# Copying the edge blocks of the normalised high bands on ScalarE instead of by transfers, in a wavelet convolution and codebook kernel

## The chip, the cores and the metric

One Trainium2 chip, one core of it. The metric is the device time of one execution in microseconds (us). The kernel before takes 2009.77 us, the median of 3 runs (2007.31 to 2010.28).

## What is computed

The input x has 8 images of 128x128 pixels with 32 channels. Two residual stages follow each other. The first normalises each channel over its image, splits the result into four half-size Haar bands, and runs three convolution branches over the three high bands:

```python
LL, LH, HL, HH = _dwt_haar(x)
hf = jnp.concatenate([LH, HL, HH], axis=-1)
x1 = _lrelu(_conv(_lrelu(_conv(hf, w15, b15)), w25, b25))
x2 = _lrelu(_conv(_lrelu(_conv(hf, w13, b13)), w23, b23))
x3 = _lrelu(_conv(_lrelu(_conv(hf, w12, b12)), w22, b22))
added = x1 + x2 + x3
y = ...                      # wd1, wd2, wd3: 3x3 convolutions, dilated by 2
alpha = jax.nn.sigmoid(_conv(y, wca, bca))
phf = alpha * hf
z = ...                      # wcb (3x3) over [LL, phf], batch norm, z * sigmoid(z)
phf2 = _conv(phf, whf, bhf)
return _idwt_haar(pLL, phf2, HL, HH)
```

The second stage normalises again and adds, for each pixel, the nearest of 512 codebook rows (argmin of the distance over 32 dimensions):

```python
x = x + _L0_conv_ref(_gn(x), ...)
x = x + _L1_conv_ref(_gn(x), L1_conv_codebook)
```

## The kernel before, in words

A half-size band is 64x64 pixels of 32 channels. On the chip a band is a tile of 128 partitions, four neighbouring columns by 32 channels, with 16 such blocks of columns (JN) by 64 rows along the free dimension, and two rows of zeros at each end. A convolution is a sum of 128x128 matrices (`wring`, `wfull`) times such a tile, shifted by rows: the matrix mixes the four columns of a block. For columns that lie in the neighbouring block there is a second tile, the EDGE tile: its lower 64 partitions hold two columns of the next block, its upper 64 two of the block before. The 5x5 convolution w15 over the three high bands reads both, OWN and EDGE.

The three high bands are kept as a rounded part and a rest, so that TensorE can multiply in its quick format (fp32r) and still be exact enough: `hf[m][kind][low]`, with m the band (3), kind OWN or EDGE, low 0 or 1, all in the one buffer `hfp`. ScalarE writes the rounded OWN parts (`normal_own`, L1174, semaphore s_hfw), VectorE the rests (`normal_low`, L1358, semaphore s_hfl), both at the end of the image before. SyncE makes the EDGE tiles by transfers within SBUF (`edges_of`, L740).

The kernel runs three images at once, in `rounds`: in round b it does the convolutions of image b, the codebook search of image b-1 (128 score products called "tile", L884, then MAX8 L1484 and FIND_INDEX8 L1488 on VectorE, then a gather of codebook rows by GpSimd, L1603), and the transform of image b+1 (transposes L816, copy L1151, Haar sums L1300 to L1305). All engines walk the same list `PLAN`, 610 steps, each doing at a step what is its part: the order of work is thus fixed for every engine, and semaphores tie them. `("mm", ...)` is one matrix product; ("tile", t), ("ychunk", c), ("xchunk", c) and ("edge", m) are set between products. The three edge steps stand at 49, 56 and 63 units of the plan's own account of TensorE (`AT`): edge 0 right behind the first product of w22, edge 1 and 2 within the OWN products of w15. The products of w15 that read EDGE tiles begin behind all 90 OWN products.

Behind the last product of a group (convolution and half) ScalarE evacuates the PSUM bank to `z` (L1044), adding the bias, and frees the bank (s_free); VectorE then applies the leaky ReLU from `z` (L1368), waiting for s_free. For w22 VectorE adds the two branches right behind it (L1374). ScalarE also does, from round to round: `lln`, the normalised low band, and its sides (L1168, L1181), at the step edge 1; the codebook search's operands, `high` (L1083) and `stack_high` (L1100), which tiles eight steps later read; and the copies of ychunk (L1162) and xchunk (L1151) that free score banks. There are four score banks, handed out in turn: a tile's product waits (`bank_free`) until the user four turns before has been read.

TensorE waits for the EDGE tiles in `inputs_ready`, at the first EDGE product of each band: L906.

```python
EDGES = ((slice(0, P // 2), slice(1, JN), slice(0, JN - 1)),
         (slice(P // 2, P), slice(0, JN - 1), slice(1, JN)))
AT = {("edge", 0): 49, ("edge", 1): 56, ("edge", 2): 63,
      ("upper",): 191, ("xsquare", 0): 137}
```

Of the kernel before, what the change touches and what calls it, by code (L numbers as in the profile page):

```python
# [14 lines left out]
ROWS = HEIGHT // 2  # L15
# [3 lines left out]
PAD = 2  # L19
# [47 lines left out]
OWN, EDGE, LEFT, RIGHT = range(4)  # L67
# [349 lines left out]
for _i, _x in enumerate(PLAN):  # L417
    if _x[0] == "mm":
# [15 lines left out]
EDGES = ((slice(0, P // 2), slice(1, JN), slice(0, JN - 1)),  # L434
         (slice(P // 2, P), slice(0, JN - 1), slice(1, JN)))
# [14 lines left out]
def conv_vq_kernel(nc, x, weights, params, codes4, codebook, ident, group_mean, part_mask, out):  # L450
    ctx = ExitStack()
    with ctx:
# [3 lines left out]
        def sem(name):  # L456
            return ctx.enter_context(nc.semaphore(name))
# [32 lines left out]
        hf = [[[hfp[:, m, kind, low] for low in range(2)] for kind in range(2)] for m in range(3)]  # L490
# [49 lines left out]
        s_hfl = sem("s_hfl")  # L540
        s_hfe = [sem(f"s_hfe{m}") for m in range(3)]
# [24 lines left out]
        s_hfw = sem("s_hfw")  # L566
# [73 lines left out]
        def raw(par, slot):  # L640

            return bands[par][:, slot // 2, :, slot % 2, :]
# [32 lines left out]
        def _(sp):  # L675
# [46 lines left out]
            def block_rows(tile, rows, js):  # L722

                return tile[rows, js].rearrange("p j i -> p (j i)").bitcast(F32)
# [7 lines left out]
                            sp.dma_start(block_rows(side[to][low], slice(q * CH, (q + 1) * CH), dst),  # L732
                                         block_rows(hf[q][OWN][low], near, src)).then_inc(s_side[low], 16)

            def edges_of(n, m):

                for low, ready in enumerate((s_hfw, s_hfl)):
                    sp.wait_ge(ready, 3 * n + m + 1)
                    for p, src, dst in EDGES:
                        sp.dma_start(block_rows(hf[m][EDGE][low], p, dst), block_rows(hf[m][OWN][low], p, src))\  # L740
                            .then_inc(s_hfe[m], 16)

            def keep_page(p):

                if PARTED[p]:
# [20 lines left out]
            def body(b, par, conv, quant, nxt):  # L766
                v = b - 1
                if conv and b:
                    sides_of(b)
                for i, step in enumerate(PLAN):  # L770
                    what = step[0]
                    if quant and what == "var2":
                        stack(v, 0)
                    elif quant and what == "bias2":
                        stack(v, 1)
                    elif quant and what == "tile":
                        t = step[1]
                        if t % JTILES == 0 and t >= JTILES and t // JTILES + 1 < JN:
                            stack(v, t // JTILES + 1)
                        if t == 7 and v:  # L780
                            store(v - 1, XCHUNKS - 1)
                        if t % CTILES == 15 and t > CTILES:
                            store(v, t // CTILES - 1)
                    elif v > 0 and what == "late" and step[1] == TILES - 1:
                        store(v - 1, XCHUNKS - 2)
                    elif conv and what == "edge":
                        edges_of(b, step[1])
                    elif nxt and what == "xchunk":
                        ahead = XCHUNKS * (b + 1) + step[1] + 2
                        if ahead < XCHUNKS * IMAGES:  # L790
                            load(ahead // XCHUNKS, ahead % XCHUNKS)
                    if conv and i in PAGE_AFTER:
                        p = PAGE_AFTER[i] + NR
                        page(NP * b + p)
                        if b == 0 and p < NP and PARTED[p]:
                            keep_page(p)
                            raw_page(SPLIT_PAGES.index(p) + 2)
                if b > IMAGES:
                    store(v - 1, XCHUNKS - 1)
# [13 lines left out]
        def _(pe):  # L813
# [86 lines left out]
            def inputs_ready(b, n, half, m, kind, low):  # L900

                if n in SPLIT:
                    if half == 0 and n == "w13" and kind == OWN:
                        pe.wait_ge(s_hfl if low else s_hfw, 3 * b + m + 1)
                    elif half == 0 and n == "w15" and kind == EDGE:
                        pe.wait_ge(s_hfe[m], 64 * (b + 1))  # L906
                    elif half == 0 and n == "w13" and kind == LEFT:
                        pe.wait_ge(s_side[low], 96 * (b + 1))
                elif n in MAKER and m == 0:
                    if kind == 0:  # L910
                        pe.wait_ge(s_leaky, len(LEAKY) * 2 * b + GROUP[MAKER[n], half] + 1)
                    elif half == 0:
                        pe.wait_ge(s_edge, len(HAS_EDGE) * b + HAS_EDGE.index(MAKER[n]) + 1)
                elif n == "wd1":
                    if kind == 0:
                        pe.wait_ge(s_sum, 2 * b + half + 1)
                    elif half == 0:
                        pe.wait_ge(s_yedge, b + 1)
                elif n == "wcb":
                    if kind != OWN:  # L920
                        if kind == LEFT and half == 0:
                            pe.wait_ge(s_pside, b + 1)
                    elif m == 0:
                        if half == 0:
                            pe.wait_ge(s_lln, b + 1)
                    else:
                        pe.wait_ge(s_phf, 6 * b + 2 * (m - 1) + half + 1)
                elif n == "whf" and m == 2:
                    pe.wait_ge(s_phf, 6 * b + 2 * m + half + 1)
# [84 lines left out]
        def _(act):  # L1014
# [150 lines left out]
            def normal_ll(n, par):  # L1165

                wait(act, s_cbmap, 4 * (n - 1) + 1)
                nc.scalar.activation(lln[:, :, PAD:PAD + ROWS], raw(par, LL), ACT.Identity, bias=shift1[:, :],  # L1168
                                     scale=scale1[:, :]).then_inc(s_lln, 1)

            def normal_own(n, par, m):
# [2 lines left out]
                nc.scalar.activation(hf[m][OWN][0][:, :, PAD:PAD + ROWS], raw(par, BANDS[m]), ACT.Identity,  # L1174
                                     bias=0.0, scale=scale1[:, :]).then_inc(s_hfw, 1)

            def ll_sides(n):

                act.wait_ge(s_lln, n + 1)
                for to, near, src, dst in SIDES:  # L1180
                    nc.scalar.copy(pside[to][SIDE_LL * CH:P, dst, PAD:PAD + ROWS],  # L1181
                                   lln[near, src, PAD:PAD + ROWS])
# [8 lines left out]
            def body(b, par, conv, quant, nxt):  # L1191
                v = b - 1
                for i, step in enumerate(PLAN):
                    what = step[0]
                    if nxt and b and i == 0:
                        for k in range(2):
                            xorder(b + 1, k)
                    if quant and what == "var2":
                        for j in range(2):
                            high(v, 1 - par, j)  # L1200
                        for part in (0, 2):
                            stack_high(v, 1 - par, 0, part)
                    elif quant and what == "bias2":
                        code_parts(v)
                    elif quant and what == "tile":
                        j, k = step[1] // JTILES, step[1] % JTILES
                        if k in (1, 3) and j + 1 < JN:
                            stack_high(v, 1 - par, j + 1, k - 1)
                        if k == 0 and j + 2 < JN:
                            high(v, 1 - par, j + 2)  # L1210
                    elif quant and what == "ychunk":
                        ycopy(v, step[1])
                    elif nxt and what == "xchunk":
                        xcopy(b + 1, step[1], BANK[step])
                    elif conv and what == "edge" and step[1] == 1:
                        normal_ll(b, par)
                        ll_sides(b)
                    elif nxt and what == "xsquare":
                        x_squares(b + 1, 1 - par, step[1])
                    elif conv and what == "wside":  # L1220
                        weighted_side(b, step[1])
                    elif conv and what == "mm":
                        for key, (_, last) in SPAN.items():
                            if last == i:
                                evacuate(b, key)
                                if key == ("wcb", 0):
                                    low_square(b, par)
                                if key in RESTORE:
                                    restore(b, par, RESTORE.index(key))
                    if nxt and i == LOW_AT:  # L1230
                        for m in range(3):
                            normal_own(b + 1, 1 - par, m)
# [541 lines left out]
```

## Time and profile before

| what | value |
|---|---|
| median of the runs | 2009.77 us |
| the profiled execution's own time | 2006.41 us |
| its span, first to last instruction | 2004.6 us |
| mean granted clock of TensorE | 0.943 |
| TensorE (PE) busy | 1855.6 us, 93% |
| VectorE (DVE) busy | 1763.2 us, 88% |
| GpSimd (POOL) busy | 1258.9 us, 63% |
| ScalarE (ACT) busy | 1011.8 us, 50% |
| transfers | 197.21 MB, mean 98 GB/s |
| the chain that ended last | PE 50%, DVE 30%, POOL 8%, issue 6%, ACT 5% |

A share of busy time is a mean over the span. The kernel has a start of about 120 us without any codebook search, eight rounds of convolutions of some 226 us each, and a tail with search alone. In a timeline a row is: start in us, length in us, engine, line, operation, what it writes and reads, how many in a row, and in brackets the idle time of the engine just before it and who ended it. An ACT row without brackets came right behind the row before; an instruction begins about 0.1 us before its predecessor's recorded end, where they are of one engine and nothing is waited for.

### The profile page before, as it was taken

What the parts mean: (1) busy time and instruction counts of PE and PEld (TensorE: products, weight loads), DVE (VectorE), ACT (ScalarE), POOL (GpSimd) and SP (SyncE); (2) the same over time, 40 slices, a digit from 0 to 9 for tenths busy, and PEclk for the clock granted to TensorE, in tenths of its full rate; (3) what the DMA queues carried; (4) which work ended last, traced back from release to release, by engine and by line L of the source; (5) the groups of instructions that cost most, each with busy time, mean ns of one, the idle gap of its engine ahead of it and who ended that gap; (6) DMA issues with size and microseconds to landing.
All of it is one profiled execution on the core that took longest, in us unless ns stands there. A gap on an engine that the chain in (4) does not pass through costs nothing.

```text
span 2004.6 us, 22679 instructions
## 1 busy us (share of the span) xinstructions
PE 1855.6 (93%) x6112; PEld 1117.6 (56%) x6112; DVE 1763.2 (88%) x3947; ACT 1011.8 (50%) x2034; POOL 1258.9 (63%) x1363
## 2 busy tenths in 40 slices
PE   7999999999999999999999999999999999985553
PEld 5654666456754666456754666556754666432221
DVE  5312799999999999999999999999999999989896
ACT  3325464646457464655456464655456353634331
POOL 1001367756778567766777567766677567767876
PEclk8999999999999999999999999999999999995555
DMA  6621463234622463234532463234532453201111
GB/s 193 189 71 48 112 161 90 70 91 123 156 77 69 115 160 100 71 88 123 156 81 70 116 156 103 71 87 125 155 82 60 107 148 94 61 19 34 35 39 31
DMA packets 135023, 197.21 MB, mean 98 GB/s; under 512 B 36976, under 2 KB 82544, under 8 KB 134896
## 3 DMA queue, kind: packets, MB, share of 16 engines
q1 hardware_dynamic: 101808, 178.40, 31.9%
q0 software_dynamic: 32768, 16.84, 5.4%
q8 instruction: 49, 0.80, 0.2%
q14 instruction: 78, 0.64, 0.1%
q10 hardware_dynamic: 320, 0.52, 0.1%
HBM read 117.52 MB, written 23.72 MB: 70 GB/s over the span
## 4 chain that ended last, share of the span: by engine, by line
PE 50%; DVE 30%; POOL 8%; issue 6%; ACT 5%; ACTq 0%; DMA 0%; POOLq 0%; DVEq 0%
PE ring L959 42%; DVE idx L1488 11%; DVE top L1484 10%; POOL vqc L1603 7%; PE score L884 6%; PE score L816 1%; ACT yst L1100 1%; ACT ha L1032 1%; DVE bands L1305 1%; POOL vqc L1617 1%; DVE hfp L1358 1%; DVE brs L1368 1%; DVE bands L1423 1%; DVE bands L1419 1%; POOL yl L1611 1%
## 5 line engine op out<-in xcount | busy, mean ns | idle before, releaser
L1603 POOL DMA_INDIRECT vqc<-in_codebook,idx x1024 | 999.4, 976 | 454.7 <-DVE idx L1488 259.4
L1484 DVE MAX8 top<-score 128x8 f32<-128x512 f32 x1024 | 690.2, 684 | 47.5 <-PE score L884 29.5
L884 PE MATMUL score<-cst,yst 98*128 98x512 f32 x1024 | 621.2, 612 | 90.8 <-DVE idx L1488 69.9
L1488 DVE FIND_INDEX8 idx<-top,score 128x8 uint32<-128x512 f32 x1024 | 703.2, 691 | 0.0
L959 PE MATMUL ring<-hfp,wring 128*128 128x512 f32 x2160 | 596.5, 411 | 3.0 <-ACT hfp L1174 3.0
L959 PEld LDWEIGHTS ring<-hfp,wring 128*128 128x128 f32 x2160 | 411.3, 191 | 116.2 <-issue 10.7
L1100 ACT CAST yst<-bands 32x256 fp32r<-32x256 f32 x1024 | 411.7, 402 | 100.9 <-PE score L884 88.6
L959 PE MATMUL ring<-ha,wfull 128*128 128x512 f32 x896 | 439.2, 597 | 5.2 <-POOL ha L1635 4.7
L884 PEld LDWEIGHTS score<-cst,yst 98*128 98x128 f32 x1024 | 205.4, 203 | 296.7 <-DVE idx L1488 176.0
L959 PE MATMUL ring<-hb,wfull 128*128 128x512 f32 x736 | 356.7, 595 | 0.0
L959 PEld LDWEIGHTS ring<-ha,wfull 128*128 128x128 f32 x896 | 168.9, 190 | 149.4 <-issue 126.3
L959 PEld LDWEIGHTS ring<-hb,wfull 128*128 128x128 f32 x736 | 138.8, 190 | 128.1 <-issue 118.2
L1044 ACT ACTIVATE z<-ring,prm 128x512 f32<-128x512 f32 x144 | 98.8, 687 | 191.9 <-PE ring L959 188.8
L1162 ACT COPY ync<-score 128x256 f32<-128x256 f32 x128 | 41.4, 375 | 229.4 <-PE score L816 148.0
L1611 POOL TENSOR_TENSOR yl<-bands,yh 128x256 fp32r<-128x256 f32 x128 | 96.6, 757 | 15.8 <-ACT yh L1083 14.0
L1635 POOL TENSOR_TENSOR ha<-ha,brs 128x512 f32<-128x512 f32 x16 | 17.5, 1116 | 140.7 <-ACT brs L1061 140.6
L959 PE MATMUL ring<-sidep,wring 96*128 96x512 f32 x384 | 103.6, 405 | 0.0
L1083 ACT CAST yh<-bands 128x256 fp32r<-128x256 f32 x128 | 51.1, 405 | 84.5 <-DVE bands L1423 83.5
L959 PE MATMUL ring<-pside,wfull 128*128 128x512 f32 x192 | 85.9, 596 | 0.0
L1151 ACT COPY xt<-score 128x512 f32<-128x512 f32 x64 | 37.1, 582 | 93.8 <-PE score L816 71.0
L959 PEld LDWEIGHTS ring<-sidep,wring 96*128 96x128 f32 x384 | 72.7, 189 | 20.2
L1617 POOL TENSOR_TENSOR vqc<-vqc,ync 128x512 f32<-128x512 f32 x64 | 82.1, 1283 | 2.7 <-DMA vqc<-in_codebook,idx 1.6
(138 smaller groups left out, 1327.5 us busy)
## 6 DMA issues: line engine op xcount, KB each, us to landing
wring<-wparts SPq DMA_DIRECT2D x119, 384.0 KB, 3.3
hfp<-hfp SPq DMA_DIRECT2D x96, 255.0 KB, 5.2
yst<-yl SPq DMA_DIRECT2D x512, 32.0 KB
vqc<-in_codebook,idx POOLq DMA_INDIRECT x1024
out<-vqc SPq DMA_DIRECT2D x128, 128.0 KB
xnat<-in_x SPq DMA_DIRECT2D x112, 128.0 KB, 3.1
wfull<-in_weights SPq DMA_DIRECT2D x32, 384.0 KB
sidep<-hfp SPq DMA_DIRECT2D x96, 127.5 KB, 3.1
```

The costliest lines, as they stand in the source:

```text
L884: nc.tensor.matmul(score[bank][:, :], yst[0:KST, j % 2, g, wp], cst[0:KST, :], start=True, stop=True).then_inc(s_tile, 1)
L959: t = nc.tensor.matmul(ring[GBANK[key]][:, :, :], w[rows], src[rows], start=(i == first), stop=(i == last))
L1044: nc.scalar.activation(z[:, g % 2], bank[:, :, :], ACT.Identity, bias=col("b" + n[1:]))\
L1083: nc.scalar.copy(yh[:, j % 2], block_of(par, j)).then_inc(s_yh, 1)
L1100: t = nc.scalar.copy(yst[part * CH:(part + 1) * CH, j % 2, g], block_of(par, j, slice(g * CH, (g + 1) * CH)))
L1151: nc.scalar.copy(xt[:, k % 2].rearrange("p w j e i -> p (w j e i)"), score[bank][:, :])\
L1162: t = nc.scalar.copy(dst[:, j], src[:, j])
L1484: nc.vector.max(top8[:, t % 4, :], score[bank][:, :]).then_inc(s_top, 1)
L1488: nc.vector.max_index(idx[:, t // CTILES % 2, t % CTILES, :], top8[:, t % 4, :], score[bank][:, :]).then_inc(s_idx, 1)
L1603: nc.gpsimd.indirect_dma_start(vqc[:, c % 2, w * CH:(w + 1) * CH], None, codebook[:, :], bass.IndirectOffsetOnAxis(idx[:, c % 2, k, 0:1], ...
L1611: nc.gpsimd.tensor_tensor(yl[:, j % 2], bands[par][:, :, j].rearrange("p w e i -> p w (e i)"), yh[:, j % 2], ALU.subtract).then_inc(s_yl, 1)
L1617: nc.gpsimd.tensor_tensor(vqc[:, c % 2, :], vqc[:, c % 2, :], ync[:, c % 2, :], ALU.add)\
```

## The change

ScalarE copies the EDGE tiles, four copies of 64 partitions x 15 blocks x 64 rows for each band: two halves of the tile, for the rounded part and for the rest. SyncE's twelve transfers per image are gone, and so is `edges_of`. s_hfe[m] now counts one per image and band, where it counted 64. ScalarE waits for s_hfl, the rests of that band.

```diff
-            def edges_of(n, m):
-
-                for low, ready in enumerate((s_hfw, s_hfl)):
-                    sp.wait_ge(ready, 3 * n + m + 1)
-                    for p, src, dst in EDGES:
-                        sp.dma_start(block_rows(hf[m][EDGE][low], p, dst), block_rows(hf[m][OWN][low], p, src))\
-                            .then_inc(s_hfe[m], 16)
-
...
-                    elif conv and what == "edge":
-                        edges_of(b, step[1])
...
-                        pe.wait_ge(s_hfe[m], 64 * (b + 1))
+                        pe.wait_ge(s_hfe[m], b + 1)
...
+            def high_edges(n, m):
+
+                act.wait_ge(s_hfl, 3 * n + m + 1)
+                for low in range(2):
+                    for p, src, dst in EDGES:
+                        t = nc.scalar.copy(hf[m][EDGE][low][p, dst, PAD:PAD + ROWS],
+                                           hf[m][OWN][low][p, src, PAD:PAD + ROWS])
+                t.then_inc(s_hfe[m], 1)
+
...
-                    elif conv and what == "edge" and step[1] == 1:
-                        normal_ll(b, par)
-                        ll_sides(b)
+                    elif conv and what == "edge":
+                        high_edges(b, step[1])
+                        if step[1] == 1:
+                            normal_ll(b, par)
+                            ll_sides(b)
```

ScalarE's queue in a middle round, from the evacuation of w23's first half on to the copy of ychunk 2. Before:

```order
L1044 ACTIVATE z<-ring,prm 128x512 [waits s_leaky,s_grp]
L1151 COPY xt<-score 128x512 [waits s_dwt,s_xT]
L1145 COPY xord<-xnat 128x256 [waits s_x1,s_xT]
L1145 COPY xord<-xnat 128x256
L1044 ACTIVATE z<-ring,prm 128x512 [waits s_leaky,s_grp] x3
L1168 ACTIVATE lln<-bands,shift,scale 128x16x64 [waits s_cbmap]
L1181 COPY pside<-lln 32x15x64 [waits s_lln]
L1181 COPY pside<-lln 32x15x64
L1083 CAST yh<-bands 128x256 [waits s_yl,s_band]
L1100 CAST yst<-bands 32x256 [waits s_tile]
L1100 CAST yst<-bands 32x256 x3
```

After (line numbers of ScalarE's part are 10 lower up to `normal_own`, 1 lower behind it; L1172 is the new copy):

```order
L1034 ACTIVATE z<-ring,prm 128x512 [waits s_leaky,s_grp]
L1172 COPY hfp<-hfp 64x15x64 [waits s_hfl]
L1172 COPY hfp<-hfp 64x15x64 x3
L1034 ACTIVATE z<-ring,prm 128x512 [waits s_leaky,s_grp] x2
L1172 COPY hfp<-hfp 64x15x64 [waits s_hfl]
L1172 COPY hfp<-hfp 64x15x64 x3
L1158 ACTIVATE lln<-bands,shift,scale 128x16x64 [waits s_cbmap]
L1180 COPY pside<-lln 32x15x64 [waits s_lln]
L1180 COPY pside<-lln 32x15x64
```

The three evacuations in a row (w23's second half, w22's two halves) are now parted behind the first by four copies; four more stand ahead of the low band, and the last four behind the next eight `yst` casts and ahead of the copy of ychunk 2:

```order
L1090 CAST yst<-bands 32x256 [waits s_tile]
L1090 CAST yst<-bands 32x256 x3
L1172 COPY hfp<-hfp 64x15x64 [waits s_hfl]
L1172 COPY hfp<-hfp 64x15x64 x3
L1152 COPY ync<-score 128x2x4x32 [waits s_add,s_yT]
L1152 COPY ync<-score 128x2x4x32
```

SyncE's queue at the same place. Before:

```order
L740 DMA hfp<-hfp 64x1020 [waits s_hfw]
L740 DMA hfp<-hfp 64x1020
L740 DMA hfp<-hfp 64x1020 [waits s_hfl]
L740 DMA hfp<-hfp 64x1020
L764 DMA wring<-wparts 128x768 [waits s_kept0,s_grp]
L740 DMA hfp<-hfp 64x1020 [waits s_hfw]
L740 DMA hfp<-hfp 64x1020
L740 DMA hfp<-hfp 64x1020 [waits s_hfl]
L740 DMA hfp<-hfp 64x1020
L719 DMA yst<-yl 32x256 [waits s_yl,s_tile]
```

After:

```order
L756 DMA wring<-wparts 128x768 [waits s_kept0,s_grp]
L719 DMA yst<-yl 32x256 [waits s_yl,s_tile]
L719 DMA yst<-yl 32x256 x3
L756 DMA wring<-wparts 128x768 [waits s_kept1,s_mark]
L756 DMA wring<-wparts 128x768 [waits s_kept2,s_mark]
```

The weight pages (`wring<-wparts`) and the operand transfers (`yst<-yl`) now stand directly behind one another. TensorE's, VectorE's and GpSimd's queues keep their order.

## Rows read from the trace of the kernel before

**Rows 1.** Page, busy time by engine, and the chain that ended last.

```profile
PE 1855.6 (93%) x6112; PEld 1117.6 (56%) x6112; DVE 1763.2 (88%) x3947; ACT 1011.8 (50%) x2034; POOL 1258.9 (63%) x1363
PE 50%; DVE 30%; POOL 8%; issue 6%; ACT 5%; ACTq 0%; DMA 0%; POOLq 0%; DVEq 0%
```

**Rows 2.** Windows of round 4: length, busy PE, PEld, DVE, ACT, POOL; clock, DMA share.

```profile
955.00:965.00 10.00, 10.00 (x44) 7.92 (x43) 10.00 (x24) 4.69 (x11) 6.10 (x7) 1.00 0.96 248
1000.00:1040.00 40.00, 39.98 (x125) 22.03 (x124) 38.76 (x88) 19.70 (x40) 29.97 (x31) 1.00 0.31 80
```

**Rows 3.** Timeline of ACT in round 4, 936 to 967 us.

```profile
936.18 4.05 ACT L1032 COPY ha<-ha 32x960 f32<-32x960 f32 x4
940.25 2.03 ACT L1032 COPY hb<-hb 32x960 f32<-32x960 f32 x2
...
946.47 0.69 ACT L1044 ACTIVATE z<-ring,prm 128x512 f32<-128x512 f32 x1
...
948.14 0.70 ACT L1044 ACTIVATE z<-ring,prm 128x512 f32<-128x512 f32 x1
949.67 0.69 ACT L1044 ACTIVATE z<-ring,prm 128x512 f32<-128x512 f32 x1 [0.84 <-PE ring L959]
952.28 0.69 ACT L1044 ACTIVATE z<-ring,prm 128x512 f32<-128x512 f32 x1 [1.92 <-PE ring L959]
952.87 1.24 ACT L1168 ACTIVATE lln<-bands,shift,scale 128x1024 f32<-128x1024 f32 x1
...
956.18 0.41 ACT L1083 CAST yh<-bands 128x256 fp32r<-128x256 f32 x1
956.49 3.31 ACT L1100 CAST yst<-bands 32x256 fp32r<-32x256 f32 x8
966.35 0.65 ACT L1162 COPY ync<-score 128x256 f32<-128x256 f32 x2 [6.54 <-PE score L816]
```

**Rows 4.** Groups by line and form, ACT: copies of the new shape, writers of hfp.

```profile
L1021 ACT COPY ha<-ha 64x960 f32<-64x960 f32 x32 | 32.3, 1009 | 18.7 <-DVE ha L1368 18.5
L1174 ACT ACTIVATE hfp<-bands,scale 128x1024 fp32r<-128x1024 f32 x24 | 25.9, 1143 | 48.9 <-DVE shift L1338 48.9
```

**Rows 5.** Timeline of DVE in round 4, then round 1, then round 7.

```profile
947.20 0.69 DVE L1368 SCALAR_TENSOR_TENSOR brs<-z 128x512 f32<-128x512 f32 x1 [1.09 <-ACT z L1044]
952.87 0.69 DVE L1368 SCALAR_TENSOR_TENSOR brs<-z 128x512 f32<-128x512 f32 x1
...
269.68 0.69 DVE L1368 SCALAR_TENSOR_TENSOR brs<-z 128x512 f32<-128x512 f32 x1
...
1629.44 0.67 DVE L1368 SCALAR_TENSOR_TENSOR brs<-z 128x512 f32<-128x512 f32 x1
1644.43 0.70 DVE L1484 MAX8 top<-score 128x8 f32<-128x512 f32 x1 [0.25 <-PE score L884]
```

**Rows 6.** Timeline of PE: the wait for DVE in round 4 and in round 7.

```profile
967.64 0.50 PE L884 MATMUL score<-cst,yst 98*128 98x512 f32 x1 [0.26 <-DVE idx L1488]
970.41 0.40 PE L884 MATMUL score<-cst,yst 98*128 98x512 f32 x1
...
1649.64 0.51 PE L884 MATMUL score<-cst,yst 98*128 98x512 f32 x1 [0.22 <-DVE idx L1488]
```

**Rows 7.** Timeline of ACT: w23's last evacuation in rounds 1 and 7.

```profile
264.95 0.70 ACT L1044 ACTIVATE z<-ring,prm 128x512 f32<-128x512 f32 x1
1624.70 1.26 ACT L1044 ACTIVATE z<-ring,prm 128x512 f32<-128x512 f32 x2
```

**Rows 8.** Timeline of DVE in round 0: the next wait behind w22.

```profile
79.82 0.36 DVE L1348 CAST wring<-ync 128x384 fp32r<-128x384 f32 x1 [1.14 <-PE ring L959]
```

**Rows 9.** Timeline of POOL in round 4; then its waits for a DMA.

```profile
961.22 0.75 POOL L1611 TENSOR_TENSOR yl<-bands,yh 128x256 fp32r<-128x256 f32 x1
POOL vqc L1617 <- DMA vqc<-in_codebook,idx: 1.6, 1, 1.6
POOL vqc L1603 <- DMA out<-vqc: 1.4, 1, 1.4
```

## The prediction

> **What bounds the kernel now.** I read the page first. TensorE is busy for 93% of the span, VectorE for 88%, ScalarE for 50%, and the chain that ended last runs through TensorE for 50% and through VectorE for 30%; transfers have 0% of it [rows 1]. So neither the removed transfers nor ScalarE, which gets the work, looks like the bound. The windows of a middle round show the two that are: from 955 to 965 us VectorE and TensorE are both busy for all 10.00 us, and from 1000 to 1040 TensorE for 39.98 of 40 [rows 2]. Two engines are nearly full and hold each other up in turn. A delay of either that is not taken up before the other waits for it goes into the end time, and once in every round. The question is therefore not how much ScalarE has to do, but whether VectorE or TensorE comes to wait for it at the three places where the copies stand.
>
> The timelines of ScalarE, VectorE and TensorE between 936 and 972 us answer that. VectorE does the leaky ReLU of w22's first half at 952.87 us, without any wait ahead of it [rows 5]: `z` had been ready since 949.67 + 0.69 = 950.36 [rows 3]. From there on it has no gap, until at 967.64 us TensorE waits 0.26 us for it, since all four score banks are full [rows 6]. So between 952.87 and 967.64 VectorE sets the pace, and behind it TensorE does, with hardly a gap up to 1040.
>
> **The change, part by part.** A copy of 64x960 takes 1009 ns on ScalarE [rows 4], and four in a row 4.05 us, with the next instruction 4.07 us behind the first's start [rows 3]. There are 3 x 4 x 8 = 96, so ScalarE gets 96 x 1.009 = 97 us more work, 1109 us in all or 55%. By itself that costs nothing.
>
> *Edge 0.* The copies stand between the evacuations of w23's second half and w22's first half. The former starts at 948.14 us; whatever follows it without a wait starts 0.59 us later (as 952.28 and 952.87 show) [rows 3]. Four copies put the evacuation of w22 to 948.14 + 0.59 + 4.07 = 952.80 instead of 949.67. VectorE's leaky ReLU starts 0.73 us behind its evacuation (946.47 to 947.20) [rows 3, 5], so at 953.53 instead of 952.87: it is late by 0.66 us. TensorE itself doesn't care: the banks that w15 takes next were freed by w23's two evacuations, which stand ahead of the copies. The second half of w22 was evacuated at 952.28 and now goes at about 953.4, while VectorE is busy with the first half and the sum of the branches, so nothing comes on top. Round 1 gives the same: 264.95 + 5.39 = 270.34 against 269.68, again 0.66 [rows 5, 7]. The plan is the same in rounds 1 to 6, which makes **6 x 0.66 = 4.0 us**.
>
> VectorE has no gap in the next 15 us to take that up in, and TensorE already waits for it at 967.64, so the wait there becomes 0.9 us and the 0.66 us goes into the end in full.
>
> *Round 7* has no transform of a next image, so VectorE comes to w22 sooner. The second of the two evacuations that start at 1624.70 begins at 1625.28; 1625.28 + 5.39 = 1630.67 against 1629.44, 1.23 us late [rows 5, 7]. VectorE has a gap of 0.25 us at 1644.43, ahead of TensorE's wait at 1649.64 [rows 5, 6], so **1.0 us** is left.
>
> *Round 0* has no search. `z` of w22 comes 2.4 us later than VectorE wants it, but VectorE waits 1.14 us for TensorE at 79.82 and over 3 us at each of the next three weight pages [rows 8], and the split pages run some pages ahead of their use. Nothing, unless that lead is smaller than it looks.
>
> *Edge 1* adds 4.07 us ahead of the low band. Going down ScalarE's queue with the lengths of the rows: w22's second evacuation 953.4 to 954.1, four copies to 958.0, `lln` and its sides to 961.35, `yh` to 961.8, eight `yst` casts to 965.0 (they ended at 959.8) [rows 3]. GpSimd wants that `yh` at 961.22, and itself comes 0.66 later now, at 961.88 [rows 9]: just in time. The tile that reads the `yst` stands behind the transposes of ychunk 2, just over 966 us. Nothing, with 0.1 us to spare at the first place and over 1 us at the second.
>
> *Edge 2* then runs from 965.0 to 968.9 and puts the copy of ychunk 2 from 966.35 to 968.9, ready at 969.6. Its score bank is wanted four turns later, by the product at 970.41 [rows 6], which itself is 0.66 later. Nothing, with 1.5 us to spare. Behind it ScalarE has gaps again and catches up. The first EDGE product of w15 stands 90 products and some 20 tiles behind 951.7, at about 977.5 us; the copies are done by 968.9, so the new form of that wait isn't felt either.
>
> *Removed.* SyncE issues 12 x 8 = 96 transfers less. They ran where the transfer engines were fullest, at a share of 0.96 [rows 2]. But no row of the steady rounds shows TensorE or VectorE waiting for a transfer; the only waits of GpSimd for one are 1.6 and 1.4 us in the whole run [rows 9]. I put the relief at nothing, with 3.0 us as its bound.
>
> **The sum** is 4.0 + 1.0 = 5.0 us, against the profiled execution's 2006.41: 2011.4. That execution is 3.4 us under the median of the runs shown, so in the terms of the median 2009.77 + 5.0 = **2014.8 us**, 0.25% more.
>
> The unknown price is that of the copy, which no row shows from `hfp` to `hfp` in fp32r. The nearest row by shape, partitions and operation is the 1009 ns that I take. The far bound is what ScalarE's writer of `hfp` takes, 1143 ns for 1024 columns and 128 partitions [rows 4]: then edge 0 is late by 4 x 0.134 = 0.54 more in seven rounds, and the sum is 5.0 + 3.8 = 8.8 us, or 2018.5. On the other side, without the 3.0 us of waits for transfers, it is 2.0 us, or 2011.8. The Trainium skill (VectorE: DVE Perf Modes, the section on the TRN2 errata) gives a ScalarE copy within SBUF 224 cycles plus one per element at 1.2 GHz: that is (224 + 960) / 1.2 = 987 ns, an estimate from that page, against the trace's 1009. By it edge 0 would be late by 0.57 us and the sum 4.4 us, just above what a measurement can tell; the trace's duration is used.
>
> **The rivals.** *Paid back* (not slower): the end hardly moves, because the delay of 0.66 us and a relief of transfers cancel. For it speaks the DMA share of 0.96 just there: the transfers that carry weight pages and `yst` now start up to 3 us sooner. Against it speaks that their readers did not wait. The most that it gives back is 3.0 of 5.0 us; if VectorE's delay were also met by gaps that the modelled ends of the products hide, nothing would be left: 2009.8 to 2011.8.
>
> *A score bank comes late* (slower still): with longer copies edge 2 pushes the copy of ychunk 2 beyond the turn of its bank. From 1.24 us a copy on (what `lln` takes) twelve copies are 12 x 0.23 = 2.8 us longer, the bank is free at 972.3 against a wish at 970.41 + 0.66 + 0.92 = 971.99, and each round loses 0.92 us at edge 0 and 0.35 at the bank: 5.0 + 7 x 1.27 = 13.9, or 2023.7. It decides from about 1.2 us a copy; below, the bank is free in time.
>
> *The transfers did hold something up* (faster): they take bandwidth from the gathers or slow the engines' own reads, and the end moves below 2005.8. Against it, no such wait is in the rows beyond the 3.0 us, which even alone, with no delay at edge 0, would give 2006.8. The Trainium skill (SBUF — State Buffer, Who interferes with whom) says that a DMA never contends with a compute engine for SBUF; by that rule nothing at all is gained there.
>
> **How the numbers follow.** A measurement of this kernel tells about 0.2% from no change, 4.0 us here. The forecast case has 0.58; since 5.0 lies only 1.0 above the bound, 0.13 of it would come out as "same". Paid back has 0.24, the late bank 0.10, the faster case 0.08. That gives slower 0.45 + 0.10 = 0.55, same 0.13 + 0.24 = 0.37, faster 0.08. The range goes from 2008.5 (paid back, with about a microsecond for the run) to 2019.0 (the far bound of the copy), and leaves out most of the late bank and of the faster case.
>
> **What would show it.** Right: 96 copies `hfp<-hfp` of 1.01 us and ScalarE near 1109 us; a wait of VectorE for `z` of about 0.66 us at w22's first half in rounds 1 to 6, where there was none, and of about 1.2 in round 7; TensorE's wait at the second tile behind ychunk 2 grown from 0.26 to 0.9 us; rounds 0.66 us longer. Wrong: rounds of the old length though VectorE waits (then it was taken up, and the place of that gap tells where); copies well over 1.01 us; a wait of TensorE for ync or `yst` around 965 to 972 us; or a wait of GpSimd for `yh` that VectorE then shows.

## The result, and the profile after

The changed kernel takes 2013.96 us (median of 19 runs, 2012.44 to 2016.08) against 2010.0 us for the kernel before, measured beside it in as many runs (2006.29 to 2013.02). The ratio is 1.0021, with a 95% interval of 1.0014 to 1.0027: slower by 4.0 us, where 5.0 had been forecast.

The page of the profiled execution, busy time by engine and the chain that ended last, answers to [rows 1]:

```profile
PE 1863.4 (93%) x6112; PEld 1118.2 (56%) x6112; DVE 1763.5 (88%) x3947; ACT 1107.2 (55%) x2130; POOL 1259.0 (63%) x1363
PE 50%; DVE 29%; POOL 8%; ACT 7%; issue 6%; ACTq 0%; DMA 0%; POOLq 0%; DVEq 0%
```

ScalarE is busy 95 us more, 1107.2 where 1109 was forecast, and TensorE 8 us more; the others are as before. The groups by line and form name the new copy (partitions x elements, count, busy us, mean ns, idle time ahead):

```profile
L1172 ACT CAST hfp<-hfp 64x960 fp32r<-64x960 f32 x96 | 97.1, 1011 | 1.0
```

It takes 1011 ns where 1009 was taken from [rows 4]. The timeline of ScalarE in round 4, to be laid beside [rows 3]:

```profile
951.35 0.69 ACT L1034 ACTIVATE z<-ring,prm 128x512 f32<-128x512 f32 x1
951.94 0.58 ACT L1141 COPY xt<-score 128x512 f32<-128x512 f32 x1
952.40 0.72 ACT L1135 COPY xord<-xnat 128x256 f32<-128x256 f32 x2
953.02 0.69 ACT L1034 ACTIVATE z<-ring,prm 128x512 f32<-128x512 f32 x1
953.60 4.06 ACT L1172 CAST hfp<-hfp 64x960 fp32r<-64x960 f32 x4
957.68 1.27 ACT L1034 ACTIVATE z<-ring,prm 128x512 f32<-128x512 f32 x2
958.84 4.09 ACT L1172 CAST hfp<-hfp 64x960 fp32r<-64x960 f32 x4
962.95 1.25 ACT L1158 ACTIVATE lln<-bands,shift,scale 128x1024 f32<-128x1024 f32 x1
...
966.27 0.41 ACT L1073 CAST yh<-bands 128x256 fp32r<-128x256 f32 x1
966.58 3.32 ACT L1090 CAST yst<-bands 32x256 fp32r<-32x256 f32 x8
969.92 4.09 ACT L1172 CAST hfp<-hfp 64x960 fp32r<-64x960 f32 x4
974.04 0.65 ACT L1152 COPY ync<-score 128x256 f32<-128x256 f32 x2
...
1010.18 0.69 ACT L1034 ACTIVATE z<-ring,prm 128x512 f32<-128x512 f32 x1 [2.88 <-PE ring L949]
```

From 953.02 on ScalarE has no gap at all up to the copy of ychunk 2. The evacuation of w22's first half starts 4.66 us behind that of w23's second half; before it was 1.53 us behind. And VectorE in the same round, and in round 7:

```profile
952.07 0.69 DVE L1369 SCALAR_TENSOR_TENSOR brs<-z 128x512 f32<-128x512 f32 x1 [1.09 <-ACT z L1034]
958.40 0.69 DVE L1369 SCALAR_TENSOR_TENSOR brs<-z 128x512 f32<-128x512 f32 x1 [0.58 <-ACT z L1034]
959.73 0.68 DVE L1369 SCALAR_TENSOR_TENSOR brs<-z 128x512 f32<-128x512 f32 x1
...
1639.27 0.69 DVE L1369 SCALAR_TENSOR_TENSOR brs<-z 128x512 f32<-128x512 f32 x1 [1.12 <-ACT z L1034]
```

The wait of 0.58 us at w22's first half is new; rounds 1 to 6 all show it. Its second half, at 959.73, is not waited for.

How long a delay lasts is best read between two fixed points of a round: from the evacuation of w23's first half to that of w15's first half, four evacuations later, 951.35 to 1010.18 here. I call this stretch S and use it below. It is 58.83 us after, and was 58.17 before: from 946.47 [rows 3] to the evacuation in this row of the kernel before.

```profile
1004.64 0.69 ACT L1044 ACTIVATE z<-ring,prm 128x512 f32<-128x512 f32 x1 [2.88 <-PE ring L959]
```

In rounds 1 to 5 it is 58.16 or 58.17 before and 58.81 or 58.82 after; in round 7 56.75 and 57.58. In round 0 it is 49.00 in both, though VectorE waits there for w22's first half too, 2.33 us: the waits of 1.14 and 3.28 us for TensorE that came behind it have shrunk to none and 2.41.

The profiled executions differ by more than the medians: their spans are 2004.6 and 2013.8 us, 9.2 us apart. Seven stretches S account for 5.3 of it (0.66 in rounds 1 to 5, 1.16 in round 6, 0.83 in round 7). Of the 1.16 only about 0.65 belongs to the change: in round 6 VectorE also waits for GpSimd (its `vqc`), 0.69 us in the kernel before and 1.17 in the changed one, but 1.18 and 1.23 us in e3 and e1 below too, which lose nothing. The rest is not in the places that the change touches. In round 0, between w15's first evacuation and the next round's, the kernel after takes 147.67 us and the one before 146.21, with as many products. Windows of that stretch, after and then before (length, busy us of PE, PEld, DVE, ACT, POOL, granted clock, DMA share):

```profile
117.88:265.55 147.67, 145.89 (x438) 79.87 (x437) 71.56 (x144) 72.87 (x122) 30.67 (x35) 0.99 0.27 75
```

```profile
117.08:263.29 146.21, 144.43 (x438) 78.82 (x437) 71.42 (x144) 72.88 (x122) 30.59 (x35) 1.00 0.29 79
```

The clock was lower for a moment, and a narrow window of the kernel after shows where:

```profile
225.00:232.00 7.00, 5.22 (x23) 3.69 (x22) 2.60 (x5) 6.37 (x17) 1.69 (x6) 1.00 0.43 135
232.00:236.00 4.00, 4.00 (x12) 3.12 (x11) 2.65 (x5) 2.06 (x6) 0.19 (x1) 0.57 0.09 27
```

From 232 to 236 us the granted clock is 0.57, that is mostly at 1.2 GHz, right behind 7 us in which TensorE was busy for 5.22 only; elsewhere in the stretch it is 2.4 GHz. Such a piece costs 1.5 us here. The profiled execution before has three in its steady rounds, this one six, and e1 and e3 below, whose times are those of the kernel before, have three and six. So of the 9.2 us about 5 are the change and about 4, by three more drops at 1.3 to 1.5 us, are an estimate for the clock; the medians of 19 runs are 4.0 us apart.

### The profile page after: what moved, and what is told of

The parts are those of the page before. It is cut to its first block, busy times and chain, and to the rows that moved or that the text cites. A ratio compares the mean times of both kernels' runs of the same rounds, so it can differ in the third digit from the quotient of the medians.

```text
span 2013.8 us, 22679 instructions
## 1 busy us (share of the span) xinstructions
PE 1863.4 (93%) x6112; PEld 1118.2 (56%) x6112; DVE 1763.5 (88%) x3947; ACT 1107.2 (55%) x2130; POOL 1259.0 (63%) x1363
## 4 chain that ended last, share of the span: by engine, by line
PE 50%; DVE 29%; POOL 8%; ACT 7%; issue 6%; ACTq 0%; DMA 0%; POOLq 0%; DVEq 0%
PE ring L949 41%; DVE idx L1489 11%; DVE top L1485 10%; POOL vqc L1604 6%; PE score L874 6%; PE score L806 1%; ACT yst L1090 1%; ACT ha L1022 1%; ACT hfp L1172 1%; DVE hfp L1359 1%; DVE bands L1306 1%; POOL vqc L1618 1%; DVE bands L1424 1%; ACT z L1034 1%; DVE bands L1420 1%
## 5 line engine op out<-in xcount | busy, mean ns | idle before, releaser
L1172 ACT CAST hfp<-hfp 64x960 fp32r<-64x960 f32 x96 | 97.1, 1011 | 1.0
```

What stands on the lines that cost most here:

```text
L1172: t = nc.scalar.copy(hf[m][EDGE][low][p, dst, PAD:PAD + ROWS], hf[m][OWN][low][p, src, PAD:PAD + ROWS])
```

## The experiments

The ten kernels of this section were each timed beside the kernel before on the same chip. The ratio is worked out from all runs and is close to that of their means, so it isn't the quotient of the medians. S is that of rounds 1 to 5 of the profiled execution; in e8, e9 and e10 the evacuation with which S begins is itself moved.

| kernel | median us | before, us | ratio, 95% interval | S, us |
|---|---|---|---|---|
| before | 2010.0 | | | 58.17 |
| changed | 2013.96 | 2010.0 | 1.0021 (1.0014 to 1.0027) | 58.82 |
| e1, band 0 by transfers | 2009.42 | 2010.96 | 0.9998 (0.9989 to 1.0007) | 58.16 |
| e2, band 0 alone by copies | 2014.78 | 2010.96 | 1.0025 (1.0016 to 1.0034) | 58.83 |
| e3, all copies, later steps | 2010.9 | 2010.96 | 0.9999 (0.9990 to 1.0008) | 58.16 |
| e4, edges in round 0 alone | 2011.54 | 2010.96 | 1.0003 (0.9994 to 1.0012) | 58.16 |
| e5, more copies at band 0 | 2029.33 | 2011.87 | 1.0091 (1.0074 to 1.0108) | 61.19 |
| e6, more copies at band 1 | 2023.56 | 2011.87 | 1.0057 (1.0038 to 1.0076) | 59.78 |
| e7, more copies at band 2 | 2023.18 | 2011.87 | 1.0061 (1.0044 to 1.0078) | 59.78 |
| e8, before, casts one tile later | 2027.51 | 2011.87 | 1.0083 (1.0068 to 1.0099) | not comparable |
| e9, before, four casts moved | 2001.87 | 2009.69 | 0.9961 (0.9949 to 0.9973) | not comparable |
| e10, e3 with the same casts moved | 2002.47 | 2009.69 | 0.9963 (0.9950 to 0.9976) | not comparable |

**Which of the three places costs: e1 and e2.** Both mix the two ways by band:

```diff
+                    elif conv and what == "edge" and step[1] in (0,):     # e2: in (1, 2)
+                        edges_of(b, step[1])
...
-                        high_edges(b, step[1])
+                        if step[1] not in (0,):                            # e2: not in (1, 2)
+                            high_edges(b, step[1])
```

> Band 0's edges by transfers as before, bands 1 and 2 by ScalarE. My theory: only the copies ahead of w22's evacuation cost anything, so VectorE doesn't wait for z at w22's first half and the time is that of the kernel before, 2010 us (within 1.5); the stretch from w23's first evacuation to w15's first evacuation is 58.2 us long in rounds 1 to 6, as before, and not 58.8. Rival, ScalarE's load as such: two thirds of the change's 4.0 us stay, 2012.7. Rival, relief by the transfers removed: under 2008.

> Band 0's edges by ScalarE, bands 1 and 2 by transfers. My theory: the whole cost is here, 2014 us as the changed kernel, VectorE's wait of 0.58 us at w22's first half in rounds 1 to 6 and a stretch of 58.8 us. Rival, load as such: one third of 4.0 us, 2011.3.

Both as the theory has it. With eight of the twelve copies in place and only band 0 back on the transfers, S is 58.16 us and the time that of the kernel before. With four of the twelve it is 58.83 and the whole loss is there; bands 1 and 2 add nothing to it in the changed kernel, where S is the same. The waits of VectorE for `z` at w22 and its neighbours, summed over the run (us, times, longest), first e1 and then e2:

```profile
DVE brs L1380 <- ACT z L1044: 20.4, 12, 3.4
```

```profile
DVE brs L1380 <- ACT z L1044: 26.8, 20, 2.9
```

In e2 there are eight waits more, one in each round, as in the changed kernel (27.0 us in 20); e1 has what the kernel before has (20.4 in 12). ScalarE's load as such is ruled out.

**The same work at other steps: e3.** The edge steps stand later in the plan:

```diff
-AT = {("edge", 0): 49, ("edge", 1): 56, ("edge", 2): 63,
+AT = {("edge", 0): 54.8, ("edge", 1): 63, ("edge", 2): 72,
```

> All edges by ScalarE, but at later steps: band 0 behind w22's second evacuation, band 1 behind the next eight yst casts, band 2 behind the copy of xchunk 2. My theory: no wait of VectorE at w22 and the time of the kernel before, 2010 us, stretch 58.2 us; the copy of ychunk 2 comes about 2.5 us later than before but ahead of its bank's turn by some 1.5 us. Rival, load as such: 2014. Rival, the bank of ychunk 2 is late: a wait of TensorE for ync and over 2011.

The low band and its sides hang on the step edge 1 and move with it. As expected, all 96 copies are on ScalarE and the time is that of the kernel before. Its timeline of ScalarE in round 4 shows the evacuations back behind one another and the copies in the gaps:

```profile
949.17 0.70 ACT L1034 ACTIVATE z<-ring,prm 128x512 f32<-128x512 f32 x1
950.68 0.69 ACT L1034 ACTIVATE z<-ring,prm 128x512 f32<-128x512 f32 x1 [0.82 <-PE ring L949]
953.29 0.69 ACT L1034 ACTIVATE z<-ring,prm 128x512 f32<-128x512 f32 x1 [1.92 <-PE ring L949]
953.88 4.09 ACT L1172 CAST hfp<-hfp 64x960 fp32r<-64x960 f32 x4
```

So what the change costs is its place in the queue, not the copies.

**What the transfers cost: e4.** The edges are made in round 0 alone, so later images use the first image's.

```diff
-                        high_edges(b, step[1])
+                        if b == 0:
+                            high_edges(b, step[1])
...
-                        pe.wait_ge(s_hfe[m], b + 1)
+                        pe.wait_ge(s_hfe[m], 1)
```

> Edge tiles are made in round 0 alone (later images read those of the first image, so this leaves out 84 of the 96 copies and all transfers). It shows what the transfers themselves cost the kernel before. My theory: nothing, 2010 us, since nobody waits for them. Rival, relief: the transfers held something up, and without them and without copies it is 3 us or more faster, 2007 or less; then the copies cost more than the 4.0 us seen.

With neither transfers nor copies the time is that of the kernel before, 2011.54 against 2010.96, and S is 58.16 as with the 96 transfers. So they cost nothing, though they ran at a DMA share of 0.96 [rows 2]. This settles the two rivals that lived on a relief. The Trainium skill's rule (SBUF — State Buffer, Who interferes with whom) is that transfers don't contend with a compute engine; the trace agrees, with S at 58.16 us with and without them.

The interval of the ratio, 0.9994 to 1.0012, leaves 1.2 us of relief open over the whole kernel; within S there is none.

**How much slack each place has: e5, e6 and e7.** Four more copies of 32x384 to a tile that nobody reads, behind those of band 0, 1 or 2:

```diff
+                if m == 0:                                                 # e6: 1, e7: 2
+                    for g in range(BLK):
+                        p = slice(g * CH, (g + 1) * CH)
+                        t = nc.scalar.copy(spare[p], hf[m][OWN][0][p, 0:6, PAD:PAD + ROWS])
                 t.then_inc(s_hfe[m], 1)
```

> The changed kernel with four more copies of 32x384 (0.51 us each by the rows, 2.05 us) right behind band 0's, written to a spare tile that nobody reads. My theory: VectorE's wait for z at w22 is already there, so every round from 1 to 7 grows by the 2.05 us in full: 7 x 2.05 = 14.4 more than the changed kernel, 2028 us, and the stretch from w23's first evacuation to w15's first is 60.9 us. Rival, VectorE takes part of it up later: under 2022.

> The same four more copies behind band 1's edges, ahead of the low band. My theory: the place has slack; yst casts end about 972.0 where the tile that reads them starts at 971.9, and the copy of ychunk 2 ends at 976.7 where its bank is wanted at 975.9, so 0 to 1 us per round in rounds 1 to 7: 2014 to 2021 us. Rival, every microsecond on ScalarE here costs one: 2028.

> The same four more copies behind band 2's edges, ahead of the copy of ychunk 2. My theory: that copy ends 2.05 us later, at 976.7, where TensorE's product wants the bank at 975.9, so 0.8 us per round at most, 2014 to 2020 us, with a wait of TensorE for ync that was not there. Rival, every microsecond on ScalarE here costs one: 2028.

The copies took 517 ns, 2.1 us in four. In e5 VectorE, whose leaky ReLU is L1374 there, waits 2.70 us at w22's first half in round 4, where the changed kernel shows 0.58: the 2.1 us in full. TensorE now waits for VectorE in one piece, at an earlier tile than in the changed kernel, and the clock falls right behind it (a timeline row of VectorE, one of TensorE, and a window of e5):

```profile
967.87 0.69 DVE L1374 SCALAR_TENSOR_TENSOR brs<-z 128x512 f32<-128x512 f32 x1 [2.70 <-ACT z L1035]
972.54 0.74 PE L875 MATMUL score<-cst,yst 98*128 98x512 f32 x1 [2.09 <-DVE idx L1494]
972.50:976.00 3.50, 3.46 (x8) 2.77 (x9) 3.50 (x9) 3.44 (x4) 2.60 (x3) 0.52 0.08 16
```

S grew by 2.37 us to 61.19, where 60.9 was expected. A drop of the clock stands in S in every round from 1 to 6; in round 7, where there is none, S grew by 2.13 us, about the length of the copies. That the other 0.24 us are the price of the drop is likely, but no run separates it. Over the seven rounds S grew by 16.4 us; the ratio went from 1.0021 to 1.0091, which is 14 us where 14.4 were expected, in an interval of some 3.4 us to either side. So the place at band 0 passes everything on, and the rival that VectorE takes part of it up, under 2022 us, is ruled out.

In e6 and e7 S grew by 0.96 us each for the same 2.1 us: both delay the same copy of ychunk 2, and about 1.1 us were free there. The expectations had some 1.2, between 974.7, the end of that copy, and the 975.9 at which its bank is wanted. The bank of ychunk 2 is what becomes late, as TensorE shows in e7, in round 4:

```profile
978.77 1.33 PE L950 MATMUL ring<-hfp,wring 128*128 128x512 f32 x5
980.84 0.50 PE L875 MATMUL score<-cst,yst 98*128 98x512 f32 x1 [0.73 <-ACT ync L1153]
```

and in e6 with 0.45 us at the same product, plus 0.50 for VectorE ahead of it, where the changed kernel has 0.34. Both medians, 2023.6 and 2023.2, lie over the upper end expected (2021 and 2020), and so do the two kernels by their ratios: 7.2 and 8.0 us over the changed kernel, where at most 7 and 6 were expected and seven times 0.96 is 6.7. The forecasts were right that these places have slack and 0.1 to 0.2 us a round too generous with it; the rival by which every microsecond costs one, 2028, is ruled out.

**A way to be faster: e8, e9, e10.** The kernel before has a wait of VectorE for `z` of 1.09 us in every round from 1 on [rows 5], at w23's first half, because ScalarE still casts `yst` for a later tile. e8 moves the last four casts of each operand but the last a tile down, e9 those of one operand behind w23's second evacuation; e10 is e9's edit on e3.

```diff
-                        if k in (1, 3) and j + 1 < JN:
-                            stack_high(v, 1 - par, j + 1, k - 1)
+                        late = 5 if j == 2 else 3                          # e8: 3 if j == JN - 2 else 4
+                        if k in (1, late) and j + 1 < JN:
+                            stack_high(v, 1 - par, j + 1, 2 * (k == late))
```

> The kernel before with the last four yst casts of an operand one tile later (tile 4 of 8 and not 3, but for the last operand), so that w23's first evacuation doesn't wait behind them. My theory: VectorE's wait of 1.09 us for z there falls away or shrinks, but TensorE, which waited 0.36 us for VectorE some 20 us later, can win no more than that: 0 to 2.5 us faster, 2007.5 to 2010. Rival, VectorE is the bound there: 7 x 1.09 = 7.6 us faster, 2002.5. Rival, an operand is late elsewhere: slower.

> The kernel before with four yst casts of one operand only (the one read from tile 24 on) moved behind w23's second evacuation. My theory: VectorE's wait of 1.09 us for z at w23's first half falls to nothing, but the stretch of 58.16 us shrinks by TensorE's waits for VectorE behind it alone, 0.36 us, to 57.8: 2.5 us in seven rounds, 2008.5 or 0.1%. Rival, VectorE sets the pace of the whole stretch: it shrinks by 1.09 to 57.1, 7.6 us in all, 2003.4. Rival, the Haar sums of VectorE come to wait for the casts: no shorter than 58.16.

> Both: all edges by ScalarE at the later steps, and the same four casts moved. My theory: what the one and the other give, stretch 57.8 us and 2.5 us less than the kernel before, so 6 us under the changed kernel. Rival, ScalarE is now too full ahead of ychunk 2: a wait of TensorE for ync and a stretch of 58.2 or more.

e8 is a miss: 2027.5 us, 0.8% slower. Its waits show a new one that no other kernel here has, VectorE's Haar sums for the casts, and in round 4 the wait for `z` has only moved on to w23's second half:

```profile
DVE sd L1301 <- ACT yst L1100: 29.2, 23, 2.4
...
962.82 0.70 DVE L1369 SCALAR_TENSOR_TENSOR brs<-z 128x512 f32<-128x512 f32 x1 [1.21 <-ACT z L1044]
```

The Haar sums overwrite the bands of the image that is being searched, so they must wait for its casts, and a cast one tile later meets them. That these 29.2 us of waits are what costs the 0.8% is argued and not tested; the third rival of the expectation is the one that fits.

e9 is a miss too, and near its first rival: 2001.87 us, a ratio of 0.9961 (0.9949 to 0.9973), 7.8 us faster than the kernel before (5.4 to 10.3) and not 2.5. The wait is gone, as VectorE shows in round 4:

```profile
944.62 0.69 DVE L1489 FIND_INDEX8 idx<-top,score 128x8 uint32<-128x512 f32 x1
945.23 0.67 DVE L1369 SCALAR_TENSOR_TENSOR brs<-z 128x512 f32<-128x512 f32 x1
```

A round without a drop of the clock, from w15's first evacuation in round 4 to that in round 5, is 224.9 us long in e9, 225.7 in the kernel before and 226.4 in the changed one. That is 0.8 us less than before, between the 0.36 of my theory and the 1.09 of the rival. I had held that TensorE could win back only what it is shown to wait for VectorE: 0.08 and 0.28 us in e3, 0.07 and 0.26 in the kernel before. TensorE at that place, before and then in e9:

```profile
965.71 0.60 PE L816 MATMUL score<-idn,bands 128*128 128x128 f32 x4
966.38 0.51 PE L884 MATMUL score<-cst,yst 98*128 98x512 f32 x1
966.72 0.67 PE L959 MATMUL ring<-hfp,wring 128*128 128x512 f32 x2
...
968.94 0.46 PE L884 MATMUL score<-cst,yst 98*128 98x512 f32 x1
```

```profile
964.92 0.60 PE L816 MATMUL score<-idn,bands 128*128 128x128 f32 x4
965.27 0.48 PE L884 MATMUL score<-cst,yst 98*128 98x512 f32 x1
965.59 0.66 PE L959 MATMUL ring<-hfp,wring 128*128 128x512 f32 x2
966.09 0.40 PE L884 MATMUL score<-cst,yst 98*128 98x512 f32 x1
...
967.29 0.49 PE L884 MATMUL score<-cst,yst 98*128 98x512 f32 x1
```

From the transposes to the third tile it is 3.23 us before and 2.37 in e9, 0.86 less, of which the row at 967.64 marks 0.26 as a wait [rows 6]. The rest lies between starts that the profile shows as busy, since the ends of products are modelled. The sum of the shown waits was no cap. The rival's 1.09 us were not all won either, because in e9 VectorE comes to wait for TensorE, where it had no gap before:

```profile
965.86 0.70 DVE L1485 MAX8 top<-score 128x8 f32<-128x512 f32 x1 [0.26 <-PE score L884]
```

Seven rounds of 0.86 us make 6.0, inside the interval of the measured 7.8.

e10 does both and gives the same, 2002.47 us: all edges on ScalarE, no transfers for them. By the ratios it is 7.4 us under the kernel before and some 12 us under the changed kernel, where 2.5 and 6 were expected, a miss for the same reason as e9. It has no advantage over e9, which keeps the transfers.

## Why the prediction was right

**The bound.** Right. The two nearly full engines hold each other up, and a delay of VectorE of 0.66 us goes into the round in full: S grew by 0.64 to 0.66 us in rounds 1 to 5, and e5 repeats it for 2.1 us more.

**The price of the copy**, 1009 ns, came out at 1011, and four in a row at 4.06 and 4.09 us. The far bound of 1143 ns was not needed. The estimate by the Trainium skill's formula (VectorE: DVE Perf Modes, the section on the TRN2 errata), 987 ns, is 2% under it.

**Edge 0, 6 x 0.66 = 4.0 us.** Right in place, cause and size; e2 alone has all of it. The wait shown is 0.58 us, since a row of VectorE that waits for nothing begins 0.08 us ahead of its predecessor's recorded end, and the wait is counted from that end; the delay is the sum of the two. The prediction had TensorE's wait growing from 0.26 to 0.9 us. It didn't. The changed kernel shows two waits there:

```profile
971.91 0.50 PE L874 MATMUL score<-cst,yst 98*128 98x512 f32 x1 [0.34 <-DVE idx L1489]
973.17 0.50 PE L874 MATMUL score<-cst,yst 98*128 98x512 f32 x1 [0.28 <-DVE idx L1489]
```

They come to 0.62 us, 0.3 more than the 0.26 and 0.07 before; the remainder of the 0.66 lies between busy rows, as in e9.

**Round 7, 1.0 us.** S grew by 0.83. The wait is 1.12 us, so with the 0.08 the delay is 1.20 where 1.23 was worked out.

**Round 0, nothing.** Right: S is 49.00 us in both, though `z` came 2.4 us late, as forecast.

**Edges 1 and 2, nothing.** Right by e1, where they are copied and cost nothing, and by e2, which has the whole loss without them. The slack left was given as 1.5 us; e6 and e7 find about 1.1. A part of the difference is a slip in the sum: four copies from 965.0 end at 969.1, by the 4.07 us used elsewhere, and not at 968.9. The case of a late bank was thus real, and some 1.1 us of ScalarE's time away. As band 0's four copies put off the bank's wish as much as the copy itself, that is 1.1 us over eight copies: an estimate of 1.15 us a copy where the prediction had 1.2, and just at its far bound of 1143 ns.

**The removed transfers, nothing.** Right by e4. With that, the case in which they pay the delay back has fallen, and so has the faster one. But the bound of 3.0 us was read from too few rows. In the kernel before GpSimd also waits for the first image's transfers at the very start, and ScalarE from round to round for the next image's:

```profile
POOL xord L1680 <- DMA bands<-in_x: 3.8, 2, 3.0
ACT xord L1145 <- DMA xnat<-in_x: 42.4, 24, 4.4
```

The latter is 36.4 us after the change. The prediction didn't look at these rows; that the edge transfers' part in such waits costs nothing is what e4 shows.

**The sum.** 5.0 us were forecast, 4.0 measured, with an interval of 2.8 to 5.4 us. The slowdown is clear of noise, but whether it is over the 0.2% that the prediction took as its bound is not: the interval runs from 0.14 to 0.27%. That the slower case came out and not "same" is in part luck. What the stretches of the profiled executions give, 6 x 0.66 + 0.83 = 4.8 us, agrees with the sum; the one microsecond between it and the medians is less than the 1.5 us that a single drop of the clock cost in round 0.

## What to carry to other kernels

An engine at half load is not free at every step: what a transfer did in no one's way becomes a block in an in-order queue, and it costs what the first consumer behind it has to wait. Look for the evacuation or the hand-over that stands right behind the place, take the time at which its reader comes for it, and put the block behind it; here three numbers in a table made the difference between 4 us lost and none. Measure such a thing between two fixed events of a round rather than by the total, and don't read the sum of the shown waits of a nearly full TensorE as the most that it can win.

## What had not been expected of the hardware

TensorE can lose time with no idle time shown. In the kernel before 0.86 us more than in e9 went by between the starts of the same products in round 4, with 0.26 us of it marked as idle by the row shown.

The drops of the clock: short pieces at the lower level, 1.2 GHz, one of them 1.5 us of loss in a stretch of 146.2 us. In the twelve traces 65 of them lie between 120 and 1780 us, from two (e10) to eleven (e5) in one execution, and each begins within 2 us of the end of a time in which TensorE was idle for 1.8 to 2.2 us. The reverse doesn't hold: the kernel before has seven such idle times and three drops. So the number differs between kernels that take the same time, but a kernel can also bring drops on itself, as e5 does: each of its six new waits of 2.1 us is followed by one. The time from w15's first evacuation to the next round's w23 in round 0 is 146.2 us in the kernel before, e2 and e3, and 147.7 in the changed kernel, e1 and e4, whose programs there hardly differ; the first three have no drop there, the others one each. This is also why one profiled execution, 9.2 us longer, would have given a wrong size.
